# Two of 56 gathered columns per chunk are fetched row by row from SP's and ScalarE's DMA queues

## The chip, the cores and the metric

The kernel runs on one core of one Trainium2 chip. The metric is the device time of that core in microseconds (us); smaller is better. The profiled execution is one run of the same program under the hardware profiler.

## The reference, cut to what matters

A graph of 6250 nodes and 200000 edges, sorted by destination. One small attention layer over the edges (layer 0, with its own scalar weights), then a graph network of three layers of edge attention with 8 heads of 8, all in float32. For the change only the three layers matter:

```
for l in range(3):
    h = layernorm(x)
    q = h[dst] @ Wq;  k = h[src] @ Wkn + edge_attr @ Wke;  v = h[src] @ Wvn + edge_attr @ Wve
    alpha = softmax over the edges of one dst of (q * k).sum per head
    agg   = segment_sum(alpha * v, dst)
    x = x + update(agg, h) @ Wout + MLP(layernorm(x))
```

So each layer needs, for each of the 200000 edges, one row of 128 floats (key and value of the node `src[edge]`), out of a table `tabkv` in DRAM that the layer computes for all nodes.

## The kernel before, in words

The edges are laid out as 128 partitions by 1568 steps (padded): partition p holds 1568 consecutive edges. A layer walks them in 28 chunks (`NCH`) of 56 steps (`C`); a chunk is 128 x 56 edges. Chunks alternate between two buffers, u = 0 and 1. The loop over chunks is written with two chunks in one iteration, on every engine. There are 3 x 28 = 84 such chunks. All orders are written out by hand, engine by engine, with semaphores between them.

For one chunk of a layer:

- **SP (the sync engine)** loads `srcI`, the 128 x 56 source node numbers (L482), once the chunk before in the same buffer has been seen (`seen1`, raised by VectorE as it starts the last slab, L1433); then the spread queries `QQ` (L486, after `q_flat`); then the transposed edge features `EA` (L490, after `done1`).
- **POOL (GpSimd)** issues 56 indirect DMAs, one per step (L546, called from L612 and L614). Each fetches 128 rows of 512 bytes of `tabkv`, one per partition, into column t of `G1[:, u, t, :]`. It may start a buffer when `done1` says that the chunk two before is finished with it.
- **TensorE** computes the edge part of key and value, in 7 slabs (`PT`) of 8 steps (L756).
- **VectorE** first spreads the queries by 8 scans (L1424), then takes the slabs one by one: it waits for the 8 gathers of a slab (L1431), adds the gathered key (L1435) and value (L1436), multiplies with the query (L1438). After the seventh slab come the reduction over heads (L1441), a running maximum, the weights, the weighted value (L1454) and nine scans of running sums (L1461), which end in `done1`.
- **ScalarE** flattens the queries of the next chunk (`query`, L959; it waits until VectorE has finished the seventh slab of this chunk), takes three exponentials (L967 to L969), waits for `done1`, copies the states into `S1` (L973) and issues their store to DRAM (L975). `edges1` is this sequence for one chunk.

Around the 28 chunks stand, in each layer, the computation of the table, a scatter of the queries by 49 indirect DMAs of POOL (L599), and the node update behind them.

Of the kernel before, what the change touches and what calls it, by code (L numbers as in the profile page):

```python
# [5 lines left out]
P = 128  # L6
N = 6250
# [35 lines left out]
B_PE, B_ACT, B_DVE = 11, 8, 5  # L43
HALVES = (range(0, 3), range(3, NB))

PD_RP, PD_END = 6, 7
# [10 lines left out]
def build(nc, A, out):  # L57
# [28 lines left out]
    with ctx:  # L86
# [3 lines left out]
        def sem(name):  # L90
            return ctx.enter_context(nc.semaphore(name))
# [85 lines left out]
        ea_in = [sem(f"ea_in{u}") for u in range(2)]  # L177
        got1 = [[sem(f"got1_{u}_{k}") for k in range(PT)] for u in range(2)]
        seen1 = sem("seen1")
        done1 = sem("done1")  # L180
# [123 lines left out]
        al1 = sb("al1", [P, H, CX])  # L304
        qb = sb("qb", [P, D])

        G1f = G1[:, :, :, :].rearrange("p u c w -> p (u c w)")
# [20 lines left out]
        def hold(eng, passed, s, value):  # L328

            eng.wait_ge(s, value)  # L330
            eng.sem_inc(passed, 1)
# [5 lines left out]
        def _(sp):  # L337
# [118 lines left out]
            with sp.Fori(0, L) as l:  # L456
# [23 lines left out]
                def sources(c, u):  # L480
                    sp.wait_ge(seen1, l * NCH + c + 1)
                    sp.dma_start(srcI[:, u, :], src_pt[:, bass.ds(c * C, C)]).then_inc(idx1[u], 16)  # L482

                def queries(c):
# [11 lines left out]
                for u in range(2):  # L496
                    sources(u, u)
                    features(u, u)
                table_weights(l + 1)
                hold(sp, waits_sp, q_put, (l + 1) * (16 * NT))  # L500
                hold(sp, waits_sp, q_first, (l + 1) * 16)
                sp.dma_start(qexp[0:EP, :].rearrange("(p t) d -> p t d", p=P)[:, 0, :], qb[:, :]).then_inc(q_done, 16)
                hold(sp, waits_sp, q_done, (l + 1) * 16)
                for u in range(2):
                    queries(u)
                with sp.Fori(1, NCH // 2) as i:
                    for u in range(2):
                        sources(2 * i + u, u)
                        queries(2 * i + u)
                        features(2 * i + u, u)  # L510

                store_fixed(st1, R1, l + 1)
# [18 lines left out]
        def _(pool):  # L531
# [62 lines left out]
            with pool.Fori(0, L) as l:  # L594
# [12 lines left out]
                with pool.Fori(0, NCH // 2) as i:  # L607
                    for u in range(2):
                        c = 2 * i + u
                        pool.wait_ge(idx1[u], l * (NCH // 2 * 16) + i * 16 + 16)  # L610
                        hold(pool, waits_pool, done1, l * NCH + c + 1)
                        gathers(u, G1, tabkv, lambda t: got1[u][t // 8], range(C // 2))  # L612
                        hold(pool, waits_pool, kv_ready, (l * NCH + c) * PT + 1)
                        gathers(u, G1, tabkv, lambda t: got1[u][t // 8], range(C // 2, C))  # L614
                fix_and_fetch(st1, R1, l + 1, [(st1_out, (l + 1) * (16 * (NCH + 1)) + 16)], rows1)
# [213 lines left out]
        def _(act):  # L829
# [122 lines left out]
            with act.Fori(0, L) as l:  # L952
# [7 lines left out]

                def edges1(c, u, ahead):

# [5 lines left out]
                    f(score8[:, :, 1:CX], score8[:, :, 1:CX], ACT.Exp, scale=SCALE).then_inc(e1_ready, 1)  # L968
                    f(gate8f, gate8f, ACT.Exp, scale=SCALE).then_inc(e1_ready, 1)  # L969
                    act.wait_ge(done1, n + 3)  # L970
                    act.wait_ge(st1_out, l * (16 * (NCH + 1)) + c * 16 + 16)
                    if ahead:
                        f(S1[:, :, :], SX[:, :, 1:CX].rearrange("p r c -> p c r"), ACT.Copy).then_inc(s_rows, 1)  # L973
                        act.wait_ge(s_rows, n + 2)
                        act.dma_start(chunk_rows(st1, R1, c), S1[:, :, :].rearrange("p c w -> p (c w)")).then_inc(st1_out, 16)  # L975
                    else:
                        f(S1[:, 0:C // 2, :], SX[:, :, 1:1 + C // 2].rearrange("p r c -> p c r"), ACT.Copy).then_inc(s_half, 1)
                        f(S1[:, C // 2:C, :], SX[:, :, 1 + C // 2:CX].rearrange("p r c -> p c r"), ACT.Copy).then_inc(s_rows, 1)
                        act.wait_ge(s_half, l + 2)
                        act.dma_start(chunk_rows(st1, R1, c)[:, 0:C // 2 * R1],  # L980
                                      S1[:, 0:C // 2, :].rearrange("p c w -> p (c w)")).then_inc(st1_out, 16)
                        act.wait_ge(s_rows, n + 2)
                        act.dma_start(chunk_rows(st1, R1, c)[:, C // 2 * R1:C * R1],
                                      S1[:, C // 2:C, :].rearrange("p c w -> p (c w)")).then_inc(st1_out, 16)

                query(l * NCH)
                with act.Fori(0, NCH // 2 - 1) as i:
                    edges1(2 * i, 0, True)
                    edges1(2 * i + 1, 1, True)
                edges1(NCH - 2, 0, True)  # L990
                edges1(NCH - 1, 1, False)
                fix_exp(V1, l + 1, SCALE)
# [21 lines left out]
        def _(dve):  # L1014
# [377 lines left out]
            with dve.Fori(0, L) as l:  # L1392
# [21 lines left out]
                with dve.Fori(0, NCH // 2) as i:  # L1414
                    for u in range(2):
# [12 lines left out]
                        for s in range(PT):  # L1428
                            b = 2 * ((u * PT + s) % 3)
                            steps = slice(8 * s, 8 * s + 8)  # L1430
                            dve.wait_ge(got1[u][s], l * (NCH // 2 * 128) + i * 128 + 128)  # L1431
                            if s == PT - 1:
                                dve.sem_inc(seen1, 1)  # L1433
# [139 lines left out]
```

## Time and profile before

| | us |
|---|---|
| median of 3 runs (9159.09 to 9161.79) | 9159.48 |
| profiled execution, its own time | 9160.98 |
| span of the profiled execution | 9159.2 |
| POOL busy | 6365.8 (70%) |
| VectorE busy | 5799.7 (63%) |
| TensorE busy | 3667.0 (40%) |
| ScalarE busy | 2862.4 (31%) |
| mean busy share of the 16 DMA engines in a stretch of the layers | 0.40 |

Busy time counts the engine's own instructions. Register, branch and semaphore instructions, and the issuing of DMAs on SP's and ScalarE's queues, are not in it; a "q" behind an engine's name (SPq, ACTq) marks its instruction queue, where such issues are listed with a duration.

### The profile page before, as it was taken

The numbers are of one execution on the slowest core, as the hardware profiler recorded it, in microseconds if no ns is written. First come the engines' busy times: TensorE is split into PE (matmuls) and PEld (weight loads), VectorE is DVE, ScalarE is ACT, GpSimd is POOL, SyncE is SP. The second block draws the span as 40 slices with busy tenths as digits, with TensorE's granted clock in tenths as the row PEclk, the third lists the DMA queues.
The fourth block names the chain that finished last, engine by engine and source line by source line (L and its number), as shares of the span: only waits on it lengthen the run. The fifth ranks groups of instructions, "written<-read, shape, count | busy, mean of one in ns | idle before, by whom it ended". The sixth has DMA issues, their size and how long they took to land.

```text
span 9159.2 us, 45368 instructions
## 1 busy us (share of the span) xinstructions
PE 3667.0 (40%) x9857; PEld 2190.5 (24%) x9857; DVE 5799.7 (63%) x6114; ACT 2862.4 (31%) x2181; POOL 6365.8 (70%) x6734
## 2 busy tenths in 40 slices
PE   2677777776323233223342232322242222223325
PEld 1333333333122122212121221222222122212212
DVE  1666666666366776676437667767744776677673
ACT  0566666666122222222222222222221222222223
POOL 6677777774577777777457777777736777777762
PEclk9988888888656566555666665665576656656557
DMA  3455555554433443444234334434314443444331
GB/s 52 161 192 180 186 179 174 175 184 148 132 131 131 139 149 131 139 140 141 64 108 148 132 132 141 147 131 139 125 49 138 139 149 131 137 141 141 131 110 48
DMA packets 405487, 1247.08 MB, mean 136 GB/s; under 512 B 196101, under 2 KB 253910, under 8 KB 360006
## 3 DMA queue, kind: packets, MB, share of 16 engines
q0 software_dynamic: 215104, 429.19, 17.4%
q1 hardware_dynamic: 169606, 468.24, 14.6%
q10 hardware_dynamic: 20736, 349.23, 9.5%
q14 instruction: 31, 0.25, 0.0%
q8 instruction: 10, 0.16, 0.0%
HBM read 808.34 MB, written 437.84 MB: 136 GB/s over the span
## 4 chain that ended last, share of the span: by engine, by line
POOL 52%; issue 20%; PE 17%; ACT 7%; DVE 2%; DMA 1%; DVEq 1%; ACTq 0%; POOLq 0%; SPq 0%
POOL G L546 49%; PE PS L696 7%; PE PS L689 6%; ACT S L910 4%; POOL qexp L599 1%; PE PS L777 1%; POOL QQ L588 1%; PE PS L781 1%; ACT hid L886 1%; PE PS L666 1%; POOL s2exp L565 1%; POOL S L552 1%; POOL G L588 1%; ACT S L851 0%; ACT L855 0%
## 5 line engine op out<-in xcount | busy, mean ns | idle before, releaser
L546 POOL DMA_INDIRECT G<-tabkv,srcI x4704 | 4438.4, 944 | 1433.6 <-issue 1433.6
L756 PE MATMUL PS<-Wkvp,EA 128*128 128x256 f32 x4704 | 1672.9, 531 | 4296.3 <-DVE PX L1438 4217.8
L756 PEld LDWEIGHTS PS<-Wkvp,EA 128*128 128x128 f32 x4704 | 1253.4, 274 | 4716.5 <-DVE PX L1438 4381.7
L546 POOL DMA_INDIRECT G<-tab,srcI x1568 | 1481.4, 945 | 571.9 <-issue 507.2
L959 ACT ACTIVATE QQ<-QQ 128x3584 f32<-128x3584 f32 x84 | 538.4, 6410 | 3313.5 <-DVE PX L1438 3063.1
L1435 DVE TENSOR_TENSOR PS<-PS,G 128x512 f32<-128x512 f32 x588 | 408.4, 695 | 1593.3 <-DMA G<-tabkv,srcI 1575.3
L973 ACT ACTIVATE S<-SX 128x4480 f32<-128x4480 f32 x81 | 663.7, 8194 | 1238.4 <-DVEq L1462 1238.4
L689 PE MATMUL PS<-xT,W1p 128*128 128x512 f32 x1568 | 768.5, 636 | 252.2 <-ACT xT L847 243.1
L1424 DVE TENSOR_TENSOR_SCAN QQ<-PS,QQ 128x456 f32<-128x456 f32 x672 | 679.4, 1082 | 207.9 <-ACT QQ L959 192.3
L1461 DVE TENSOR_TENSOR_SCAN SX<-PS,SX 128x456 f32<-128x456 f32 x756 | 763.2, 1082 | 12.2
L696 PE MATMUL PS<-hid,W2p 128*128 128x512 f32 x1568 | 710.9, 596 | 34.2 <-ACT hid L886 31.5
L1438 DVE TENSOR_TENSOR PX<-PS,QQ 128x512 f32<-128x512 f32 x588 | 624.6, 1062 | 43.8
L886 ACT ACTIVATE hid<-PS,b1c 128x512 f32<-128x512 f32 x784 | 489.1, 684 | 300.6 <-PE PS L689 300.6
L1454 DVE TENSOR_TENSOR SX<-G,PS 128x3584 f32<-128x3584 f32 x84 | 525.7, 6258 | 87.8 <-ACT PS L968 87.8
L689 PEld LDWEIGHTS PS<-xT,W1p 128*128 128x128 f32 x1568 | 318.7, 205 | 660.4 <-issue 396.8
L1436 DVE TENSOR_TENSOR G<-PS,G 128x512 f32<-128x512 f32 x588 | 399.4, 679 | 0.0
L696 PEld LDWEIGHTS PS<-hid,W2p 128*128 128x128 f32 x1568 | 284.4, 190 | 342.0 <-issue 227.7
L910 ACT ACTIVATE S<-S 128x7336 f32<-128x7336 f32 x27 | 360.5, 13352 | 0.0
L599 POOL DMA_INDIRECT qexp<-PX,startI x147 | 140.9, 958 | 312.2 <-DVEq L1412 268.3
L1441 DVE TENSOR_REDUCE al<-PX 128x448 f32<-128x3584 f32 x84 | 326.6, 3888 | 7.7
L666 PE MATMUL PS<-ident,xe 128*128 128x128 f32 x784 | 132.0, 296 | 363.0 <-DVE xe L1188 363.0
L894 ACT ACTIVATE eaC<-PS,b2c 128x512 f32<-128x512 f32 x196 | 134.7, 687 | 418.8 <-PE PS L696 418.8
(311 smaller groups left out, 4090.8 us busy)
## 6 DMA issues: line engine op xcount, KB each, us to landing
st<-S ACTq DMA_DIRECT2D x81, 2240.0 KB, 7.8
EA<-eaT SPq DMA_DIRECT2D x84, 1792.0 KB, 7.8
QQ<-qexp SPq DMA_DIRECT2D x84, 1792.0 KB, 7.3
st<-S ACTq DMA_DIRECT2D x27, 3668.0 KB, 12.0
G<-tabkv,srcI POOLq DMA_INDIRECT x4704, 2.5
xe<-in_edge_attr SPq DMA_DIRECT2D x28, 1792.0 KB, 8.1
qexp<-zeros SPq DMA_DIRECT2D x28, 1792.0 KB, 12.6
eaT<-eaC ACTq DMA_DIRECT2D x28, 1792.0 KB
```

What stands on the lines that cost most here:

```text
L546: nc.gpsimd.indirect_dma_start(out=G[:, u, t, :], out_offset=None, in_=tab[:, :], in_offset=IND(ap=srcI[:, u, t:t + 1], axis=0)).then_inc( ...
L689: last = mm(PS[:, 1 + 2 * r + kh, :], W1p[:, r, kh, :], xT8[:, :], start=True, stop=True)
L696: last = mm(PS[:, 5, :], W2p[:, kh, r, :], hid8[:, r, kh, :], start=(r == 0 and kh == 0), stop=(r == 1 and kh == 1))
L756: last = mm(PS[:, b + j // 2, 2 * P * (j % 2):2 * P * (j % 2) + 2 * P], EA[:, u, 4 * s + j, :], Wkvp[:, :], start=True, stop=True)
L886: f(hid8[:, r, kh, :], PS[:, 1 + 2 * r + kh, :], ACT.Relu, bias=b1c[:, kh:kh + 1]).then_inc(m_act, 1)
L910: f(S0r[:, :, :], SY[:, :, 1:CX].rearrange("p r c -> p c r"), ACT.Copy).then_inc(s0_rows, 1)
L959: f(Qf[:, :, 1:CX], Q1.rearrange("p c d -> p d c"), ACT.Copy).then_inc(q_flat, 1)
L973: f(S1[:, :, :], SX[:, :, 1:CX].rearrange("p r c -> p c r"), ACT.Copy).then_inc(s_rows, 1)
L1424: scan(rows, gate8f, rows, 0.0, ALU.mult, ALU.add)
L1438: tt(PR[:, steps, :], kv_of(b)[:, :, 0:D], Qf[:, :, 1 + 8 * s:9 + 8 * s].rearrange("p d t -> p t d"), ALU.mult).then_inc(kv_used, 1)
L1454: tt(SX[:, 2 * H:R1, 1:CX].rearrange("p (j h) x -> p j h x", h=H), G1[:, u, :, D:2 * D].rearrange("p t (h d) -> p d h t", h=H), score8[:, ...
L1461: scan(rows, gate8f, rows, 0.0, ALU.mult, ALU.add)
```

## The change

POOL gathers columns 0 to 53 of each chunk (`PLAIN = C - 2 = 54`). Column 54 is fetched by SP and column 55 by ScalarE's queue, each with 128 plain DMAs, one per partition, of one row of 512 bytes. The DRAM address of each is computed from a node number that the engine reads into a register: 16 numbers by one call of `values_load_multi_w_load_instructions`, so 8 such calls and 128 DMAs per engine and chunk. To have the numbers in one partition, SP fetches for each chunk two more small arrays `lastI` (128 numbers each). The rows of a chunk are cut into quarters of 32. The quarters 0 to 2 of chunk c + 2 are issued in the iteration of chunk c, by ScalarE behind the store of the states and by SP behind the load of the features; quarter 3 of chunk c + 1 is issued in the iteration of chunk c too, by ScalarE right behind the three exponentials and by SP right behind the load of the queries. Ahead of the loop, both engines issue all four quarters of chunk 0 (SP before it stores `qb` and loads the first queries, ScalarE before its first `query`) and three of chunk 1. VectorE waits, ahead of the seventh slab, for the six gathers left in it and for the eight row semaphores.

```diff
+QUARTER = P // 4
+PLAIN = C - 2
+LAST_GOT = 16 * (PLAIN - 8 * (PT - 1))
...
                 def sources(c, u):
                     sp.wait_ge(seen1, l * NCH + c + 1)
                     sp.dma_start(srcI[:, u, :], src_pt[:, bass.ds(c * C, C)]).then_inc(idx1[u], 16)
+                    for e in range(2):
+                        sp.dma_start(lastI[0:1, u, e, :], src_pt[:, bass.ds(c * C + PLAIN + e, 1)].rearrange("p o -> o p"),
+                                     allow_slow_non_contiguous=True).then_inc(last_in[u], 16)
+
+                def plain_rows(u, i, quarters):
+
+                    hold(sp, waits_sp, last_in[u], l * (NCH // 2 * 32) + i * 32 + 32)
+                    for q in quarters:
+                        for p0 in range(q * QUARTER, (q + 1) * QUARTER, 16):
+                            _, nodes = nc.values_load_multi_w_load_instructions(
+                                lastI[0:1, u, 0, p0:p0 + 16], engines=(mybir.EngineType.SP,), min_val=0, max_val=NP - 1,
+                                skip_runtime_bounds_check_because="src holds node numbers below N")
+                            for p, node in enumerate(nodes, p0):
+                                sp.dma_start(G1[p:p + 1, u, PLAIN, :], tabkv[bass.ds(node, 1), :]).then_inc(plain_got[0][u][q], 16)
...
                 table_weights(l + 1)
+                plain_rows(0, 0, range(4))
                 hold(sp, waits_sp, q_put, (l + 1) * (16 * NT))
...
                 for u in range(2):
                     queries(u)
+                plain_rows(1, 0, range(3))
                 with sp.Fori(1, NCH // 2) as i:
                     for u in range(2):
                         sources(2 * i + u, u)
                         queries(2 * i + u)
+                        plain_rows(1 - u, i - 1 + u, range(3, 4))
                         features(2 * i + u, u)
+                        plain_rows(u, i, range(3))
+                plain_rows(1, NCH // 2 - 1, range(3, 4))
...
-                        gathers(u, G1, tabkv, lambda t: got1[u][t // 8], range(C // 2, C))
+                        gathers(u, G1, tabkv, lambda t: got1[u][t // 8], range(C // 2, PLAIN))
...
     # ScalarE, edges1; its plain_rows is SP's with act, column PLAIN + 1 and plain_got[1]
                     f(gate8f, gate8f, ACT.Exp, scale=SCALE).then_inc(e1_ready, 1)
+                    if ahead:
+                        plain_rows(1 - u, i + u, range(3, 4))
                     act.wait_ge(done1, n + 3)
...
                         act.dma_start(chunk_rows(st1, R1, c), S1[:, :, :].rearrange("p c w -> p (c w)")).then_inc(st1_out, 16)
+                        if two_ahead:
+                            plain_rows(u, i + 1, range(3))
...
+                for k in range(2):
+                    hold(act, waits_act, a_out[k], (l + 1) * (16 * ((NB + 1 - k) // 2)))
+                hold(act, waits_act, h_out, (l + 1) * 32)
+                plain_rows(0, 0, range(4))
                 query(l * NCH)
+                plain_rows(1, 0, range(3))
...
-                            dve.wait_ge(got1[u][s], l * (NCH // 2 * 128) + i * 128 + 128)
-                            if s == PT - 1:
+                            if s < PT - 1:
+                                dve.wait_ge(got1[u][s], l * (NCH // 2 * 128) + i * 128 + 128)
+                            else:
+                                dve.wait_ge(got1[u][s], l * (NCH // 2 * LAST_GOT) + i * LAST_GOT + LAST_GOT)
+                                for q in range(4):
+                                    for e in range(2):
+                                        dve.wait_ge(plain_got[e][u][q], l * ROW_SEM + i * (16 * QUARTER) + 16 * QUARTER)
                                 dve.sem_inc(seen1, 1)
```

## Rows read from the trace of the kernel before

**Rows 1.** The page's costliest groups: busy, mean ns | idle before, releaser.
```profile
L546 POOL DMA_INDIRECT G<-tabkv,srcI x4704 | 4438.4, 944 | 1433.6 <-issue 1433.6
L1435 DVE TENSOR_TENSOR PS<-PS,G 128x512 f32<-128x512 f32 x588 | 408.4, 695 | 1593.3 <-DMA G<-tabkv,srcI 1575.3
```

**Rows 2.** Timeline of SP's queue, four periods of a layer: start us, us, queue.
```profile
3038.53 0.34 SPq L482 DMA_DIRECT2D srcI<-in_src  x1
...
3318.17 0.34 SPq L482 DMA_DIRECT2D srcI<-in_src  x1
```

**Rows 3.** Timeline of ScalarE over one chunk.
```profile
3740.16 6.45 ACT L959 ACTIVATE QQ<-QQ 128x3584 f32<-128x3584 f32 x1 [37.17 <-DVE PX L1438]
...
3748.10 0.54 ACT L967 ACTIVATE SX<-PS 128x448 f32<-128x448 f32 x1 [1.49 <-DVE PS L1452]
...
3749.00 0.52 ACT L969 ACTIVATE PS<-PS 128x456 f32<-128x456 f32 x1
...
3764.79 8.19 ACT L973 ACTIVATE S<-SX 128x4480 f32<-128x4480 f32 x1 [15.28 <-DVEq L1462]
...
3773.14 0.34 ACTq L975 DMA_DIRECT2D st<-S  x1
```

**Rows 4.** Timeline of VectorE behind the seventh slab and into the next chunk.
```profile
3739.07 1.06 DVE L1438 TENSOR_TENSOR PX<-PS,QQ 128x512 f32<-128x512 f32 x1
...
3755.51 9.08 DVE L1461 TENSOR_TENSOR_SCAN SX<-PS,SX 128x456 f32<-128x456 f32 x9
...
3774.98 0.68 DVE L1435 TENSOR_TENSOR PS<-PS,G 128x512 f32<-128x512 f32 x1
...
3777.30 0.69 DVE L1435 TENSOR_TENSOR PS<-PS,G 128x512 f32<-128x512 f32 x1
...
3779.64 0.69 DVE L1435 TENSOR_TENSOR PS<-PS,G 128x512 f32<-128x512 f32 x1
```

**Rows 5.** Timeline of SP's queue at the program's start (L392: one row, 320 bytes).
```profile
12.94 0.52 SPq L389 DMA_DIRECT2D st<-zeros  x1
...
13.94 1.12 SPq L391 DMA_DIRECT2D st<-zeros  x1
15.10 0.26 SPq L392 DMA_DIRECT2D st<-zeros  x1
15.40 0.25 SPq L393 DMA_DIRECT2D st<-zeros  x1
```

**Rows 6.** Timeline of SP's queue, DMAs back to back, address from a register.
```profile
6922.73 0.55 SPq L365 DMA_DIRECT2D Wqkv<-in_Wvn  x1
6923.38 0.54 SPq L383 DMA_DIRECT2D bqkv<-in_bq  x1
...
6925.23 0.38 SPq L383 DMA_DIRECT2D bqkv<-in_bke  x1
6925.71 0.38 SPq L383 DMA_DIRECT2D bqkv<-in_bve  x1
```

**Rows 7.** All instructions of L482: durations min/median/max in ns.
```profile
L482 SPq FUSED_REGOPS  x78: 37/37/42, 2549.1 to 8768.7; - x78
L482 SPq MOVE srcI<-in_src x78: 29/29/29, 2549.2 to 8768.7; - x78
```

**Rows 8.** All DMAs of L486 and L502, and for L502 the time to landing.
```profile
L486 SPq DMA_DIRECT2D QQ<-qexp x84: 332/333/343, 2480.7 to 8777.8; - x84
...
L502 SPq DMA_DIRECT2D qexp<-qb x3: 343/344/354, 2479.1 to 6951.0; - x3
...
DMA to landing us min/median/max: 1.5/1.5/1.6
```

**Rows 9.** Timeline of all engines at the start of the third layer's chunks.
```profile
6914.39 1.19 SPq L490 DMA_DIRECT2D EA<-eaT  x1
...
6949.81 0.97 POOL L546 DMA_INDIRECT G<-tabkv,srcI  x1 [0.30 <-issue]
...
6952.64 14.11 SPq L486 DMA_DIRECT2D QQ<-qexp  x2
...
6960.14 6.25 ACT L959 ACTIVATE QQ<-QQ 128x3584 f32<-128x3584 f32 x1 [83.56 <-DMA QQ<-qexp]
...
7023.63 6.39 ACT L959 ACTIVATE QQ<-QQ 128x3584 f32<-128x3584 f32 x1 [57.24 <-DVE PX L1438]
```

More of the change, by code:

```diff
@@ L44 @@
 HALVES = (range(0, 3), range(3, NB))
+QUARTER = P // 4
+ROW_SEM = 16 * QUARTER * (NCH // 2)
+PLAIN = C - 2
+LAST_GOT = 16 * (PLAIN - 8 * (PT - 1))
 PD_RP, PD_END = 6, 7
@@ L178, in build @@
         got1 = [[sem(f"got1_{u}_{k}") for k in range(PT)] for u in range(2)]
+        last_in = [sem(f"last_in{u}") for u in range(2)]
+        plain_got = [[[sem(f"plain_got{u}_{q}_{e}") for q in range(4)] for u in range(2)] for e in ("sp", "act")]
+        waits_act = sem("waits_act")
         seen1 = sem("seen1")
@@ L305, in build @@
         qb = sb("qb", [P, D])
+        lastI = sb("lastI", [1, 2, 2, P], i32)
         G1f = G1[:, :, :, :].rearrange("p u c w -> p (u c w)")
@@ L959, in query, with plain_rows, edges1 @@
                     f(Qf[:, :, 1:CX], Q1.rearrange("p c d -> p d c"), ACT.Copy).then_inc(q_flat, 1)
-                def edges1(c, u, ahead):
+                def plain_rows(u, i, quarters):
+                    hold(act, waits_act, last_in[u], l * (NCH // 2 * 32) + i * 32 + 32)
+                    for q in quarters:
+                        for p0 in range(q * QUARTER, (q + 1) * QUARTER, 16):
+                            _, nodes = nc.values_load_multi_w_load_instructions(
+                                lastI[0:1, u, 1, p0:p0 + 16], engines=(mybir.EngineType.Activation,), min_val=0, max_val=NP - 1,
+                                skip_runtime_bounds_check_because="src holds node numbers below N")
+                            for p, node in enumerate(nodes, p0):
+                                act.dma_start(G1[p:p + 1, u, PLAIN + 1, :], tabkv[bass.ds(node, 1), :]).then_inc(plain_got[1][u][q], 16)
+                def edges1(c, u, ahead, i, two_ahead):
                     n = l * NCH + c
@@ L984, in edges1 @@
                                       S1[:, C // 2:C, :].rearrange("p c w -> p (c w)")).then_inc(st1_out, 16)
+                for k in range(2):
+                    hold(act, waits_act, a_out[k], (l + 1) * (16 * ((NB + 1 - k) // 2)))
+                hold(act, waits_act, h_out, (l + 1) * 32)
+                plain_rows(0, 0, range(4))
                 query(l * NCH)
+                plain_rows(1, 0, range(3))
                 with act.Fori(0, NCH // 2 - 1) as i:
[L988 to L991, printed above, removed]
+                    edges1(2 * i, 0, True, i, True)
+                    edges1(2 * i + 1, 1, True, i, True)
+                edges1(NCH - 2, 0, True, NCH // 2 - 1, False)
+                edges1(NCH - 1, 1, False, NCH // 2 - 1, False)
                 fix_exp(V1, l + 1, SCALE)
```

## The prediction

> **What bounds the kernel now.** I read the page's groups first. POOL's gathers of the layers are the largest: 4704 of them, 944 ns busy each, and 1433.6 us of idle time before them, all put down to issue, so POOL waits for nobody [rows 1]. That is (4438.4 + 1433.6) / 4704 = 1.248 us per gather. Then I took the period of a chunk from SP's queue: four periods are 3318.17 - 3038.53 = 279.64 us, so 69.9 us each [rows 2], and 56 x 1.248 = 69.9. POOL's issue is the whole period; VectorE waits for gathers, 1575.3 us in all [rows 1].
>
> Next, how much room the other engines have. VectorE ends the seventh slab at 3740.13 (call it T), its nine scans at 3764.6, begins the next slabs at 3774.98 and takes one per 2.33 us when nothing is missing [rows 4], so it could have the next T at 3774.98 + 7 x 2.33 = 3791.3, 51 us after this one. ScalarE [rows 3] works 6.45 (queries), three exponentials ending at 3749.52, 8.19 (states) and 0.34 (store), and sits idle 37.17 us before the queries and 15.28 us before the states. SP's queue does three DMAs per chunk. So without two gathers POOL's period would be 67.4 us, and VectorE allows it.
>
> **The change, part by part.**
>
> *POOL.* Two gathers fewer: 2 x 1.248 = 2.5 us per chunk, 84 chunks: -210 us, if nothing else becomes longer than 67.4 us.
>
> *ScalarE's queue.* It gains 128 DMAs and 8 register loads per chunk, issued in order between its activations; a DMA issue holds the queue. Call x the all-in time per row. When ScalarE is the one that is late, its loop over one chunk is: queries 6.45, exponentials 1.42, 32 rows beside the 15.27 us that VectorE needs up to `done1` (hidden while 32x stays under 15.27), states and store 8.19 + 0.15 + 0.34, small gaps 0.1 [rows 3], then 96 rows with nothing of its own chain beside them. A = 31.9 + 96x. Behind the waiting rows stand the next chunk's queries and exponentials, on which VectorE waits. The question is whether A stays below 67.4 (x below 0.370) or at least below 69.9 (x below 0.396).
>
> *The price x.* The trace has no row DMA into SBUF from a register address, and no register load at all. Issue: a single-row DMA took 0.26 us, next one 0.30 us after it (L392), two earlier single-row ones 0.52 and 1.12 [rows 5]. A 128-row DMA takes 0.333 alone [rows 8]. With a register address, DMAs back to back follow with a gap of 0.10 (6925.23 + 0.38 to 6925.71) [rows 6], in which 37 + 29 ns of register operations lie [rows 7]. So one row costs 0.26 + 0.10 = 0.36 from the nearest kind, 0.43 if it costs what 128 rows do, and 0.64 by L365's rows (0.55 and the gap). I take 0.36: L392 is the same shape, and L389 and L391 stand behind a large store. Register load of 16: below, one register operation, 0.03 us (x = 0.36), or 16 of them, 0.46 us (x = 0.385); above, a round trip of a small DMA, 1.5 us [rows 8] (x = 0.45). A load must bring its values back before the next instruction, so it is nearer to a round trip; I take 1.25 us, 0.08 per row: x = 0.435.
>
> Two of the pages bear on that load. The Trainium skill says in "Runtime: NRT & Kernel Launch" (Instruction fetch mechanics) that loading sequencer registers from HBM costs about 200 ns per register even in bulk; taken for these loads from SBUF as an estimate that is 3.2 us per 16, x = 0.56 and, by the sum below, about 10560 us. In "DMA: Bandwidth & Descriptors" (Latency and other measured facts) it gives a floor of about 600 ns for such a load, which would make x = 0.395 and leave the time where it was. No row of this trace shows either.
>
> *The sum.* A = 31.9 + 96 x 0.435 = 73.7 us, 3.8 longer than now. 32x = 13.9 is hidden.
>
> *SP.* 128x = 55.7 plus five DMAs (three as now, two of `lastI` like L365's at 0.6) is about 58 us, under 73.7: not a bound. Its order: the rows stand before the feature load and the next sources; features are needed a chunk later, sources 67 us later, and queries are asked for at T + 6.4. Cost nothing; that cover would be gone at x above 0.5, when ScalarE is worse anyway.
>
> *The start of a layer* [rows 9]. SP is done with its loads at 6926.1; with four more small loads at 6928.6; 128 rows bring it to 6984.3; `qb` goes out and lands 1.5 us later, so the first queries are asked for at 6986 instead of 6952.6 and land 7.5 us later. ScalarE's flatten ends at 6999.8, VectorE's scans and seven slabs put the first T at 7026 instead of 7023.6. ScalarE then issues 96 rows and is free at 7041.6. From the start of its loop to the next T there are 7.9 + 15.3 + 10.2 + 16.4 = 49.8 us [rows 3, 4]. So the last T of the layer is at 7041.6 + 26A + 49.8; now it is 7023.6 + 27 x 69.9. The difference is 26 (A - 69.9) - 2.1: with A = 73.7, +96.7 us per layer, three layers +290. That is against the profiled execution, 9161.0: 9451 us. It stands 1.5 us above the median of the runs, so nothing to correct.
>
> *VectorE* gets eight more waits per chunk. They are passed long before where ScalarE is early; their handling lies in VectorE's free 16 us (67.4 - 51). Nothing. The DMA engines carry 256 packets of 512 bytes in place of two gathers' worth of the same bytes; nothing at this share (0.40 busy).
>
> **The rivals.**
>
> *Cheap rows (the other side): faster.* The place is the same 96 rows of ScalarE, behind the states' store. If x is below 0.370 (row 0.36, load under 0.2 us, or a row cheaper than L392's), A stays below 67.4 and POOL remains the bound: -210 us and a few us of start, 8955 us. Between 0.370 and 0.396 a part is left: x = 0.385 gives A = 68.9, -28 per layer, 9077 us. For it: one register address costs 66 ns only, and 0.26 is the duration of L392 and of L393 [rows 5, 7]. Against it: every register load must cost nearly nothing. It decides at x = 0.396.
>
> *Dear rows.* The issue costs what a 128-row DMA does, 0.43 + 0.08 = 0.51. Then 32 rows no longer hide: A = 16.6 + 128 x 0.51 = 81.9, +310 per layer, 10090 us. The same follows from a row at 0.36 and a load of 2.4 us, that is if each of the 16 values makes a trip of its own. For it: all isolated DMAs with registers are 0.333 or more [rows 8], and values may be read one by one. The page's 200 ns per register belongs here too.
>
> *Very dear rows.* L365's pace, 0.64 + 0.08 = 0.72 [rows 6]: A = 108.8, +1009 per layer, 12190 us. For it: DMAs in bursts there cost 0.55 where isolated ones cost 0.33, and the change is one long burst from two queues at once. Against it: L392 and L393 stand back to back at 0.30 [rows 5].
>
> *It does not do what it says*: POOL's gathers become slower by contention with the row DMAs, so that 54 take 69.9 us. 1.248 is steady under all present traffic [rows 1]; I give it no chance of its own.
>
> **How the numbers follow.** Forecast (A from 70.4 to 79, +40 to +650 us): 0.36. Cheap rows, whole or partly: 0.31. Dear rows, up to +1500: 0.19. Very dear: 0.10. In between, within 0.2% of before (about what a measurement of this kernel can tell from no change): 0.04. Faster 0.31, same 0.04, slower 0.65. The range runs from the full gain, 8950, to 10500: it leaves out the very dear rows and some of the dear ones. The forecast's own range is 9200 to 9810.
>
> **What would show it.** ScalarE's queue with 128 DMAs per chunk at 0.36 us spacing within a 16 and a pause of 1.25 us between them; the period of L973 at 73.7 us against POOL's 67.4 of issue and 6 us of waiting for `done1`; ScalarE's idle time before L959 gone. The forecast is wrong if the period is 67.4 and POOL still has no wait but issue, or if rows come at 0.5 us or more.

## The result: 12% slower, and the profile after

| | us |
|---|---|
| before, median of 4 runs (9158.25 to 9161.79) | 9159.28 |
| after, median of 4 runs (10278.35 to 10286.43) | 10283.02 |
| after over before, 95% interval | 1.1226 (1.1207 to 1.1246) |
| profiled execution of after, its own time | 10286.43 |

The change costs 1124 us where 290 were forecast. These are lines of the page of the changed kernel: the chain by engine and line, then costliest groups (busy, mean ns | idle before, releaser).

```profile
span 10284.6 us, 112432 instructions
...
ACTq 37%; PE 15%; issue 13%; ACT 13%; DVE 8%; DVEq 7%; POOL 3%; SPq 2%; DMA 1%; POOLq 0%
ACTq L997 28%; ACTq L993 9%; PE PS L723 7%; DVEq L1514 6%; ACT S L1013 6%; PE PS L716 5%; DVE SX L1506 5%; ACT S L937 3%; DVE SX L1513 1%; SPq L504 1%; PE PS L804 1%; POOL QQ L615 1%; PE PS L808 1%; ACT hid L913 1%; POOL G L573 1%
...
L573 POOL DMA_INDIRECT G<-tabkv,srcI x4536 | 4279.6, 943 | 2612.5 <-issue 1351.9
...
L1506 DVE TENSOR_TENSOR SX<-G,PS 128x3584 f32<-128x3584 f32 x84 | 525.8, 6259 | 2701.4 <-ACT PS L1006 2701.4
L986 ACT ACTIVATE QQ<-QQ 128x3584 f32<-128x3584 f32 x84 | 524.4, 6243 | 4648.3 <-issue 4267.0
```

The gathers (L573) take 943 ns each, as before, and are the 168 fewer that the change asks for, but of POOL's 2612.5 us of idle time before them only 1351.9 are still issue [rows 1]: POOL waits now. VectorE waits 2701.4 us for ScalarE's exponential (L1006) ahead of the weighted value (L1506), where the kernel before has 87.8 us (L1454 there):

```profile
L1454 DVE TENSOR_TENSOR SX<-G,PS 128x3584 f32<-128x3584 f32 x84 | 525.7, 6258 | 87.8 <-ACT PS L968 87.8
```

ScalarE sits idle 4267.0 us before the queries (L986) and no engine releases it there: its own queue is busy, with the rows (L997, 28% of the chain) and the register loads (L993, 9%). This is ScalarE's timeline over one chunk, which answers to [rows 3]:

```profile
4007.46 6.26 ACT L986 ACTIVATE QQ<-QQ 128x3584 f32<-128x3584 f32 x1 [52.01 <-issue]
4009.01 4.76 ACTq L997 DMA_DIRECT2D G<-tabkv  x12
4013.63 0.52 ACT L1005 ACTIVATE SX<-PS 128x448 f32<-128x448 f32 x1
...
4014.51 0.49 ACT L1007 ACTIVATE PS<-PS 128x456 f32<-128x456 f32 x1
4014.70 8.46 ACTq L997 DMA_DIRECT2D G<-tabkv  x18
4030.29 8.19 ACT L1013 ACTIVATE S<-SX 128x4480 f32<-128x4480 f32 x1 [15.29 <-DVEq L1514]
4038.64 0.39 ACTq L1015 DMA_DIRECT2D st<-S  x1
4042.86 47.16 ACTq L997 DMA_DIRECT2D G<-tabkv  x96
4092.82 6.24 ACT L986 ACTIVATE QQ<-QQ 128x3584 f32<-128x3584 f32 x1 [54.33 <-issue]
```

From the store at 4038.64 to the next queries at 4092.82 there are 54.2 us, in which 96 rows with their six loads are issued and nothing else. The part from the queries to the store takes 31.2 us, as the prediction had it. The loop is then 85.4 us here and 83.0 us in the next chunk. This loop, from one copy of the states (L1013, before: L973) to the next, is the period of a chunk. Over the 78 periods inside the layers it is 84.14 us on the mean (69.90 before, worked out from all executions of the copy). The whole difference can be laid out from these: 6563.3 - 5452.2 = 1111.1 us in the periods, +23.7 up to the first of them, +8.8 between the layers, -18.1 behind the last; together 1125.5, which is the difference of the two spans (10284.63 and 9159.15).

What the rows and loads cost, by their lines in the trace (durations min/median/max in ns; L997 and L993 on ScalarE's queue, L504 and L500 on SP's):

```profile
L997 ACTq FUSED_REGOPS  x10752: 37/37/37, 2445.8 to 10002.2; - x200
L997 ACTq MOVE G<-tabkv x10752: 29/29/29, 2445.8 to 10002.2; - x200
L997 ACTq DMA_DIRECT2D G<-tabkv x10752: 228/235/1085, 2445.9 to 10002.3; - x200
...
L993 ACTq TENSOR_LOAD <-lastI x672: 1191/1304/3646, 2444.5 to 9994.4; - x168
```
```profile
L504 SPq DMA_DIRECT2D G<-tabkv x10752: 224/225/1167, 2456.9 to 9994.2; - x200
...
L500 SPq TENSOR_LOAD <-lastI x672: 1133/1232/3922, 2455.4 to 9986.3; - x168
```

A row is 0.037 + 0.029 for its address and 0.235 for the DMA, and with the three gaps between these instructions the next row starts 0.391 us later (median). The load of 16 takes 1.304 us; the forecast had 1.25.

### The profile page after: what moved, and what is told of

Its sections match the earlier page's. It is cut to its first block, busy times and chain, and to the rows that moved or that the text cites. A ratio compares the mean times of both kernels' runs of the same rounds, so it can differ in the third digit from the quotient of the medians.

```text
span 10284.6 us, 112432 instructions
## 1 busy us (share of the span) xinstructions
PE 3287.2 (32%) x9857; PEld 1953.7 (19%) x9857; DVE 5779.7 (56%) x6114; ACT 2839.8 (28%) x2181; POOL 6208.8 (60%) x6566
## 4 chain that ended last, share of the span: by engine, by line
ACTq 37%; PE 15%; issue 13%; ACT 13%; DVE 8%; DVEq 7%; POOL 3%; SPq 2%; DMA 1%; POOLq 0%
ACTq L997 28%; ACTq L993 9%; PE PS L723 7%; DVEq L1514 6%; ACT S L1013 6%; PE PS L716 5%; DVE SX L1506 5%; ACT S L937 3%; DVE SX L1513 1%; SPq L504 1%; PE PS L804 1%; POOL QQ L615 1%; PE PS L808 1%; ACT hid L913 1%; POOL G L573 1%
## 5 line engine op out<-in xcount | busy, mean ns | idle before, releaser
L573 POOL DMA_INDIRECT G<-tabkv,srcI x4536 | 4279.6, 943 | 2612.5 <-issue 1351.9
L783 PE MATMUL PS<-Wkvp,EA 128*128 128x256 f32 x4704 | 1299.9, 439 | 5856.5 <-DVE PX L1490 5771.7
L783 PEld LDWEIGHTS PS<-Wkvp,EA 128*128 128x128 f32 x4704 | 1019.1, 222 | 6138.0 <-DVE PX L1490 5884.9
L1506 DVE TENSOR_TENSOR SX<-G,PS 128x3584 f32<-128x3584 f32 x84 | 525.8, 6259 | 2701.4 <-ACT PS L1006 2701.4
L573 POOL DMA_INDIRECT G<-tab,srcI x1568 | 1481.7, 945 | 567.2 <-issue 510.7
L986 ACT ACTIVATE QQ<-QQ 128x3584 f32<-128x3584 f32 x84 | 524.4, 6243 | 4648.3 <-issue 4267.0
L1013 ACT ACTIVATE S<-SX 128x4480 f32<-128x4480 f32 x81 | 663.7, 8193 | 1239.2 <-DVEq L1514 1239.2
```

Of the source, the lines that this page charges most:

```text
L573: nc.gpsimd.indirect_dma_start(out=G[:, u, t, :], out_offset=None, in_=tab[:, :], in_offset=IND(ap=srcI[:, u, t:t + 1], axis=0)).then_inc( ...
L783: last = mm(PS[:, b + j // 2, 2 * P * (j % 2):2 * P * (j % 2) + 2 * P], EA[:, u, 4 * s + j, :], Wkvp[:, :], start=True, stop=True)
L1506: tt(SX[:, 2 * H:R1, 1:CX].rearrange("p (j h) x -> p j h x", h=H), G1[:, u, :, D:2 * D].rearrange("p t (h d) -> p d h t", h=H), score8[:, ...
```

## The experiments

The later runs were made on seven chips. On five of them the kernel before itself took 10846 to 10868 us, on the two others 9158 to 9160 us; no chip showed both, and what differs between them is not known. Each comparison is with the kernel before on the same chip, and only those beside 9159 us are used for sizes.

**POOL's part by itself.** The kernel before with the last two gathers of each chunk left out, and with `G1` cleared once ahead of the layers, which is not in the diff shown.

```diff
-                        gathers(u, G1, tabkv, lambda t: got1[u][t // 8], range(C // 2, C))
+                        gathers(u, G1, tabkv, lambda t: got1[u][t // 8], range(C // 2, C - 2))
```

> The kernel before with 54 gathers per chunk and nothing in place of the last two (their columns hold stale rows; G1 is cleared once, some 8 us). Theory: what the change could win at most is 2 x 1.248 us per chunk, 84 chunks, 210 us: 10650 where the kernel before takes 10855. Rival (something else paces the chunks on this chip, so that fewer gathers win nothing): 10850 or more.

Measured: 8954.21 us, 0.9775 (0.9759 to 0.9792). The page's group and two executions of the states' copy in ScalarE's timeline:

```profile
L546 POOL DMA_INDIRECT G<-tabkv,srcI x4536 | 4280.3, 944 | 1382.2 <-issue 1382.2
...
3993.55 8.19 ACT L973 ACTIVATE S<-SX 128x4480 f32<-128x4480 f32 x1 [15.29 <-DVEq L1467]
...
4060.93 8.19 ACT L973 ACTIVATE S<-SX 128x4480 f32<-128x4480 f32 x1 [15.30 <-DVEq L1467]
```

The period is 4060.93 - 3993.55 = 67.4 us and POOL waits for nothing but issue. So the removed gathers bring 204 us (9158.37 - 8954.21) where the forecast had 210, in a kernel that also clears `G1` once (6.7 us of VectorE), and what the fetching adds is about 1124 + 204 = 1328 us.

**POOL out of the way.** The changed kernel with only 7 of the 54 gathers of a chunk, one per slab. VectorE's waits are set to match, which the diff leaves out.

```diff
-                        gathers(u, G1, tabkv, lambda t: got1[u][t // 8], range(C // 2))
+                        gathers(u, G1, tabkv, lambda t: got1[u][t // 8], range(0, C // 2, 8))
...
-                        gathers(u, G1, tabkv, lambda t: got1[u][t // 8], range(C // 2, PLAIN))
+                        gathers(u, G1, tabkv, lambda t: got1[u][t // 8], range(C // 2 + 4, PLAIN, 8))
```

> The changed kernel, but POOL issues only 7 of its 54 gathers per chunk, one per slab, so that its gathers are out of the way (most edges get a stale row; G1 is cleared once, some 8 us). Theory (ScalarE's queue is the bound by its own instructions; what lengthens it further on this chip is POOL's gathers in flight): the period falls from 134.2 us in the changed kernel on this chip to 82 to 85 us, the 84.1 us of the first measurement, and the time from 15580 to about 11300. Rival (the rows themselves are slow on this chip): period stays over 120 us. Rival (POOL's gathers were part of the bound of 84.1 us too): period under 78 us.

Measured: 10232.16 us, 1.117 (1.1152 to 1.1189). Its gathers, POOL's busy tenths, and ScalarE's 96 rows:

```profile
POOL 7677777753000000001300000000040000000001
...
L573 POOL DMA_INDIRECT G<-tabkv,srcI x588 | 554.5, 943 | 6163.3 <-DVEq L1516 4165.8
...
4033.24 46.58 ACTq L997 DMA_DIRECT2D G<-tabkv  x96
```

POOL is nearly silent in the layers and the 96 rows still take 46.6 us; the period is 83.51. The period of 82 to 85 us held; the total in the expectation was that for the chips on which the kernel before takes 10850 us. Neither POOL's gathers nor contention of their transfers with the rows makes the loop: ScalarE's own stream of instructions does, but for 0.6 us of 84.1.

**Which rows count.** 32 rows more beside the stretch in which ScalarE waits for VectorE, 32 fewer behind the store: 64 and 64.

```diff
-                        plain_rows(1 - u, i + u, range(3, 4))
+                        plain_rows(1 - u, i + u, range(2, 4))
...
-                            plain_rows(u, i + 1, range(3))
+                            plain_rows(u, i + 1, range(2))
```

> 64 of ScalarE's rows ahead of its wait for done1, 64 behind the store; base 10283 us. Theory (its own order is the bound): 10.4 us more than is free there, 16.8 saved behind the store, period 78 us, 9800 us. Rival (only the sum of the rows counts): 10283.

Measured: 9719.76 us, 1.0611 (1.0593 to 1.0629), period 77.26. ScalarE's timeline:

```profile
4033.30 6.24 ACT L986 ACTIVATE QQ<-QQ 128x3584 f32<-128x3584 f32 x1 [36.00 <-issue]
...
4040.54 24.41 ACTq L997 DMA_DIRECT2D G<-tabkv  x50
4065.20 8.24 ACT L1013 ACTIVATE S<-SX 128x4480 f32<-128x4480 f32 x1 [24.36 <-issue]
...
4077.51 31.46 ACTq L997 DMA_DIRECT2D G<-tabkv  x64
```

The 64 rows beside VectorE now end at 4064.95, so that the copy of the states (L1013) waits 24.36 us and for issue, no longer for VectorE; about 9 us of them lie on the path (the part from the queries to the store is 40.3 us for 31.2) and the rest, some 23, stays hidden. Behind the store 32 rows fewer save 16 us (36.95 for 52.96); the sum is the 7 us by which the period is shorter. The rival, that only the number of rows counts, fell. In the changed kernel the rows beside VectorE are free, as forecast, because VectorE needs its 15.3 us and the rows begin already while the queries are being flattened.

**Half as many rows.** One column of 128 rows, of which SP's queue fetches 64 and ScalarE's 64 (32 behind the store, 32 beside VectorE); POOL gathers 55. The diff shows SP's start and ScalarE's rows behind the store.

```diff
-PLAIN = C - 2
+PLAIN = C - 1
...
-                plain_rows(0, 0, range(4))
+                plain_rows(0, 0, range(2))
...
-                            plain_rows(u, i + 1, range(3))
+                            plain_rows(u, i + 1, range(2, 3))
```

> One column, 64 rows by SP and 64 by ScalarE, POOL gathers 55; for a chip on which the kernel before takes 9158 us. Theory: ScalarE's loop is 84.1 - 64 x 0.52 = 51 us, SP's under 40, POOL's 68.7 holds: 9158 - 105 = 9053 us. Rival (rows cost something by being there): 9158 or more.

Measured: 9050.62 us, 0.9879 (0.9863 to 0.9896). It is 1.2% faster than the kernel before. The group of the gathers, the chain by engine, and ScalarE's timeline:

```profile
POOL 52%; issue 20%; PE 17%; ACT 7%; DVE 2%; DMA 1%; DVEq 1%; ACTq 0%; POOLq 0%; SPq 0%
...
L571 POOL DMA_INDIRECT G<-tabkv,srcI x4620 | 4359.3, 944 | 1408.8 <-issue 1408.8
...
4023.09 15.70 ACTq L995 DMA_DIRECT2D G<-tabkv  x32
4055.01 6.37 ACT L984 ACTIVATE QQ<-QQ 128x3584 f32<-128x3584 f32 x1 [35.88 <-DVE PX L1488]
```

POOL is the bound again, at 55 x 1.248 = 68.6 us (measured 68.66), and ScalarE, done with its 32 rows at 4038.8, waits again for VectorE until 4055.01. One gather per chunk is worth 109 us when the rows are hidden.

**The parts of the price.** Two kernels take parts of a row's cost away. In the first the rows come from addresses known at compile time: no load, no address operations. The diff is ScalarE's; SP's is the same with its own addresses.

```diff
-                            _, nodes = nc.values_load_multi_w_load_instructions(
-                                lastI[0:1, u, 1, p0:p0 + 16], engines=(mybir.EngineType.Activation,), min_val=0, max_val=NP - 1,
-                                skip_runtime_bounds_check_because="src holds node numbers below N")
-                            for p, node in enumerate(nodes, p0):
-                                act.dma_start(G1[p:p + 1, u, PLAIN + 1, :], tabkv[bass.ds(node, 1), :]).then_inc(plain_got[1][u][q], 16)
+                            for p in range(p0, p0 + 16):
+                                act.dma_start(G1[p:p + 1, u, PLAIN + 1, :], tabkv[41 * p:41 * p + 1, :]).then_inc(plain_got[1][u][q], 16)
```

> 256 row DMAs per chunk at constant addresses, no loads, no arithmetic (the two columns hold wrong rows). Theory: 0.30 us per row (as e4's trace shows between POOL's bursts), 96 of them 29 us, ScalarE's loop 31.9 + 29 + some 3 for store and loop end = 64 us, POOL's 67.4 us bound: 8955 us. Rival (row DMAs as such are the bound): near 10280.

Measured: 9176.46 us, 1.0016 (1.0006 to 1.0026), where the theory said 8955. In the second only the first load of each call is kept, and its 16 numbers serve for all rows of the call.

```diff
-                            _, nodes = nc.values_load_multi_w_load_instructions(
...
+                            if p0 == quarters[0] * QUARTER:
+                                _, nodes = nc.values_load_multi_w_load_instructions(
...
```

> One load of 16 numbers per call of plain_rows, reused (wrong rows for most edges); base 10283 us. Theory: 5 loads fewer behind the store, 5 x 1.53 = 7.7 us, period 76.5, 9680 us. Rival (the loads are not on the path): 10283.

Measured: 9238.12 us, 1.0079 (1.0062 to 1.0095), where the theory said 9680. Both miss, and in opposite directions. All the DMAs of the rows, and two runs of 96 rows behind the store, first of the kernel with constant addresses:

```profile
L991 ACTq DMA_DIRECT2D G<-tabkv x10752: 215/283/4347, 2448.5 to 8891.0; - x200
...
4004.99 36.04 ACTq L991 DMA_DIRECT2D G<-tabkv  x96
...
4072.97 40.51 ACTq L991 DMA_DIRECT2D G<-tabkv  x96
```

and then of the kernel with one load per call:

```profile
L999 ACTq DMA_DIRECT2D G<-tabkv x10752: 222/228/1092, 2444.4 to 8971.2; - x200
L999 ACTq FUSED_REGOPS  x2640: 37/37/37, 2444.2 to 8964.9; - x189
...
4025.73 36.51 ACTq L999 DMA_DIRECT2D G<-tabkv  x96
...
4062.53 6.24 ACT L987 ACTIVATE QQ<-QQ 128x3584 f32<-128x3584 f32 x1 [39.98 <-issue]
```

What each interval between starts on ScalarE's queue came to, from the store to the next queries, mean over the chunks inside the layers (worked out from the starts of the instructions; the row interval behind a load holds the load):

```
                         after          one load per call    constant addresses
row to row           90 x 0.426 = 38.3   95 x 0.373 = 35.4    95 x 0.393 = 37.3
over a load           6 x 1.837 = 11.0    1 x 2.503 =  2.5    none
row to load           5 x 0.264 =  1.3    none                none
store to first; last row to queries  2.3  2.5                 1.8
all                              53.0    40.4                39.1
```

With one load per call the 16 registers recur, and the program computes the address of a repeated one only once: its FUSED_REGOPS are 2640 in place of 10752. The stretch is 12.5 us shorter. The theory had 7.7 of these: five loads and the slower row behind each. It had not that the load behind the store would be shorter too, 2.35 us on the mean in place of 3.33 (1.0), nor the two rows behind that load (1.0), and nothing for the missing address operations, which the remaining 2.8 or so are put down to.

With constant addresses half of ScalarE's rows come 0.314 us or less after the one before, and yet the mean behind the store is 0.393: the DMA instructions themselves grow, to a median of 283 ns and up to 4347, where with address operations between them the median was 235. They don't grow evenly. From 4 to 8 us after the start of the states' store ScalarE's rows are 0.305 us apart on the mean, from 12 to 16 us 0.763, and from 20 us on 0.37 to 0.45; SP's rows slow down in the same microseconds (0.77 to 1.05 from 4 to 16 us). So 0.393 is the mean of this kernel and not a floor that one queue has by itself. The other queue's rows are not needed for it either: with none of SP's issued within 1.5 us, ScalarE's still come 0.374 us apart. The same kernel on the other chips shows SP's rows 0.30 us apart where neither a row of ScalarE's nor a gather is issued within 1.5 us, 0.35 with ScalarE's rows near, and 0.43 with both (all worked out from the starts of the instructions). What holds the issue back was not separated further; a kernel with one queue at constant addresses was not run. At its mean ScalarE's loop is 31.2 + 39.1 = 70.3 us (the period is 70.53), above POOL's 67.4: even rows without any load or address did not make this split faster than before.

**On the chips where the kernel before takes 10850 us.** The same kernels there, and one queue at a time: ScalarE alone with one column, and SP alone with one column (POOL gathers 55). The diff is the first one's, which takes SP's calls away; the other takes ScalarE's.

```diff
-                        plain_rows(1 - u, i - 1 + u, range(3, 4))
...
-                        plain_rows(u, i, range(3))
...
-                                    for e in range(2):
+                                    for e in (1,):
```

> SP's column goes back to POOL (55 gathers, 68.7 us per chunk); ScalarE keeps its 128 rows. Theory (ScalarE's own queue is the bound, 84.2 us per chunk in the changed kernel): same period, 10280 us. Rival (the two queues slow each other, or all rows crowd on shared DMA hardware): rows get cheaper with one queue alone, period under 80 us, under 9950 us.

> ScalarE's column goes back to POOL (55 gathers, 68.7 us); SP keeps 128 rows. Theory: SP's queue needs 8 loads and 128 rows, 67.0 us at the changed kernel's means (0.433 us per row, 1.45 per load), and some 3.7 us of other DMAs, waits and loop end: 70.7 us per chunk, about 9225 us (9160 to 9300). Rival (SP has room, as the prediction had it): POOL's 68.7 us hold, 9055 us. Rival (SP is a second bound near 84 us): over 10000 us.

The split column and the constant addresses, whose diffs stand above, were run with these two for the first time:

> One column only, 64 of its rows by SP and 64 by ScalarE (32 beside VectorE's chain, 32 behind the store of the states); POOL gathers 55. Theory: ScalarE's loop is about 84.2 - 64 rows x 0.52 = 51 us plus waits, SP's under 40, both under POOL's 68.7: 1.25 us per chunk are won, 9160 - 105 = 9055 us. Rival (plain rows cost something by merely being there, contention or waits of VectorE): no gain, 9160 or more.

> All 256 row DMAs stay, but at constant addresses of the table: no register loads, no address arithmetic (the two columns hold wrong rows). Theory (the price is load plus arithmetic plus issue, 0.52 us per row, of which the DMA itself is 0.235 and a gap): ScalarE's loop falls to about 60 us, POOL's 67.4 us bound again, 8955 us. Rival (the row DMAs themselves, their descriptors or landing, are the bound): stays near 10280 us.

The next runs were to tell whether the chip or the kernels made these times: the two kernels of the case again, and the experiments again.

> The kernel before, unchanged, with its trace, beside which all experiments are now read: it took 10846 us in two sets of experiments and 9159 us in the first measurement. If the sequencers' records there come 0.70 us apart in long stretches, as in e1's trace, the difference of 1690 us is in those stretches; if not, the DMAs or the clock are slower. If the time is 9159 us again, the set is comparable with the first measurement.

> The changed kernel, unchanged, as the base for the experiments on this chip. If it is near 10283 us, the set compares directly. If it is far above (e1 with half of its row DMAs took 15000 us), the same cause that lengthens the kernel before by 1690 us lengthens long runs of sequencer instructions, and the experiments must be read against this run.

> The kernel of e1 again, for the same reason. Theory (ScalarE's queue alone is the bound): 10280 us, 84 us per chunk. Rival (the two queues slow each other): under 9950 us.

> The kernel of e3 again, since in its first run the kernel before took 10846 us beside it and not 9159, so that neither theory could be read. Theory: both queues are under POOL's 68.7 us per chunk, 9055 us. Rival (plain rows cost something by being there): 9160 or more.

> The kernel of e4 again (256 row DMAs per chunk at constant addresses, so the two columns hold wrong rows), for the same reason. Theory (load and arithmetic are half of the price): about 60 us on ScalarE, POOL's 67.4 us bound, 8955 us. Rival (the row DMAs themselves are the bound): near 10280 us.

And the first runs of one load per call, and of 64 rows behind the store and 64 beside VectorE:

> Row DMAs with register addresses as in the change, but only one load of 16 numbers per call of plain_rows, reused for all its rows (wrong rows for most edges): 4 loads per chunk and engine fewer on the average, of 1.30 us and 0.23 us on the first row behind each. Theory (loads are part of ScalarE's 84.2 us): behind the store 5 loads fewer, 7.7 us, period 76.5 us, 10283 - 78 x 7.7 = 9680 us where the kernel before takes 9159; where it takes 10850, at least 600 us under the changed kernel's 15580. Rival (rows' issue waits for the DMA hardware, not for the loads): less than 200 us.

> ScalarE issues 64 rows (not 32) before it waits for done1, and 64 (not 96) behind the store. Theory (ScalarE's own order is the bound; 23 us lie free there from the start of the queries to done1): 64 rows take 33.4 us, 10.4 more than is free, but 16.8 are saved behind the store: period 84.2 - 6.3 = 78, about 9800 us where the kernel before takes 9159. Rival (only the sum of the rows counts): no change, 10283.

Measured:

```
                              us        over before (95% interval)
before again               10868.15    1.00 (10856 beside it)
after again                15582.34    1.4352 (1.4311 to 1.4394)
ScalarE's column alone     14993.57    1.3832 (1.3808 to 1.3855); again 1.3838 (1.3815 to 1.3862)
SP's column alone          15002.15    1.3828 (1.3805 to 1.3851); again 1.3909 (1.3886 to 1.3932)
64 and 64 behind/beside    14783.34    1.3630 (1.3607 to 1.3653)
one load per call          14318.86    1.3198 (1.3176 to 1.3220)
one column split           12968.17    1.1962 (1.1943 to 1.1982); again 1.1964 (1.1943 to 1.1984)
constant addresses         12911.15    1.1911 (1.1891 to 1.1931); again 1.1922 (1.1902 to 1.1942)
```

A run of the changed kernel there, ScalarE's queue:

```profile
L997 ACTq DMA_DIRECT2D G<-tabkv x10752: 2/235/1509, 3304.7 to 15285.0; - x200
...
6006.24 6.24 ACT L986 ACTIVATE QQ<-QQ 128x3584 f32<-128x3584 f32 x1 [104.55 <-issue]
6007.91 4.62 ACTq L997 DMA_DIRECT2D G<-tabkv  x11
...
6041.59 97.64 ACTq L997 DMA_DIRECT2D G<-tabkv  x96
6139.50 6.24 ACT L986 ACTIVATE QQ<-QQ 128x3584 f32<-128x3584 f32 x1 [102.23 <-issue]
```

The rows beside the queries come 11 in 4.62 us, as fast as elsewhere (12 in 4.76), the 96 behind the store in 97.6 us in place of 47. In the first stretch POOL is waiting, in the second it gathers. In all runs of this kind that fetch rows there are stretches in which the instructions of the two queues come 0.7 or 1.4 us apart, and they lie beside POOL's gathers. An interval between two of ScalarE's rows with no gather starting within 1.5 us of it had a median of 0.390 us in that run, one with a gather 2.1 us. That the gathers cause it is not shown: no kernel without them was run on such a chip.

ScalarE's column alone answers to the rival that the two queues slow each other. Where no gather was near, its rows came 0.535 us apart on the mean with SP silent and with SP issuing alike, so the rival finds nothing there; over the whole chunk the period fell from 134.2 to 127.0 us. The totals can't tell for the chips beside 9159 us.

The split column, 1.2% faster beside 9159, is 20% slower here, and constant addresses, no change there, are 19% slower. Among the kernels that fetch rows these two change places in the order, and the kernel before is ahead of both.

A last run of SP's column alone, meant for a chip where the kernel before takes 9159 us, met the other kind:

> SP fetches one column (128 rows and 8 loads per chunk), ScalarE's queue fetches nothing, POOL gathers 55 columns. Theory (the price of a row is the same on SP's queue, and SP's 128 rows are its own loop): in the changed kernel SP issued its rows in stretches of 14.4 and 50.1 us per chunk, and its other work and waits for itself came to about 7 us, so one turn of SP takes 70 to 72 us, against POOL's 55 x 1.248 = 68.6. The period is then 70.0 to 72.0 and the time 9170 to 9330, ScalarE's queue having none of it. Rival 1 (the prediction's figure, SP takes about 58 us): POOL stays the bound, period 68.7, time 9055, as with the column split between the queues. Rival 2 (two queues slow each other, so one alone is quick): rows at 0.36 or less, period 68.7 as well, but the spacing of rows would show it.

15115.19 us; so whether SP alone would be a bound there stays open as a total.

## Why the prediction was wrong

**POOL's gain: right.** 210 forecast, 204 measured with the two gathers left out.

**The mechanism: right.** ScalarE's loop of 31.9 + 96x was forecast; 31.2 + 53.0 was measured, with nothing in the second term but the stretch from the store to the queries; the 96 rows are on the path and the 32 are not, shown by moving 32 of them; a chunk's period sets 1111 of the 1125 us. Put into the prediction's own sum, the measured A of 84.14 gives 26 x 14.24 - 2.1 = 368 us per layer and 10265 us in all, beside 10286 of the profiled execution. The side on which it would fall was the likelier of the two given (0.65).

**The price x: wrong, and this is the step that failed.** It was 0.435, of which 0.36 for a row and 0.08 for its share of a load. By the table above, 16 rows with their load take 15 x 0.426 + 1.837 + 0.264 = 8.49 us, 0.530 each; with what stands at the end of the stretch, (84.1 - 31.9) / 96 = 0.544. A was 10.4 us short by it, 811 us over 78 periods, of the 834 us by which the change cost more than the 290 forecast. The forecast's own range, 9200 to 9810, ended below the measured time. This is the term of the rival "dear rows" (0.51 and more, chance 0.19), whose price came true though not its form: it had the 32 rows on the path too. The 10.4 us of A that were missing (84.1 less 73.7):

- The row. Its DMA cost 0.235, even less than the 0.26 of [rows 5]. But the gap of 0.10 from [rows 6] was misread: the prediction put both register operations of [rows 7] into it, 37 + 29 ns, and the trace of the kernel before has only the one of 29 ns there. These DMAs have no address to compute:

```profile
L383 SPq DMA_DIRECT2D bqkv<-in_bve x4: 381/382/432, 28.0 to 6925.7; - x4
...
L383 SPq MOVE bqkv<-in_bve x3: 29/29/29, 2456.2 to 6925.6; - x3
```

  A row of the change has both, so that 0.156 lies between the end of one DMA and the start of the next, two operations of 66 ns and three gaps of 30. Median 0.391 where 0.36 was forecast: 3.0 us per chunk.
- The load, 1.304 for 1.25: 0.3 us. The estimate between a register operation and a round trip was good. The Trainium skill's 200 ns per register ("Runtime: NRT & Kernel Launch", Instruction fetch mechanics) would be 3.2 us; this load is from SBUF and took 0.08 per register. The Trainium skill's floor of about 600 ns ("DMA: Bandwidth & Descriptors", Latency and other measured facts) is passed by a factor of two.
- The row behind a load costs 0.23 more than another (0.624 us to the next, 0.391 otherwise, medians): six times 0.23, 1.4 us. Not in the forecast.
- The load behind the states' store takes 3.33 us on the mean of 78 in place of 1.30, and the two intervals from the second and the third row behind it 0.91 and 0.87 in place of 0.39: 3.0 us. The forecast priced each instruction as if it stood alone. The place in the queue is not what makes this load slow, for SP's queue shows the same in the same microsecond. These are ScalarE's load behind the store of 4038.64, SP's load of that moment, and SP's load right behind its own DMA of 128 rows, the features:

```profile
L993 ACTq TENSOR_LOAD <-lastI x1: 3252/3252/3252, 4039.2 to 4039.2; - x1
...
L500 SPq TENSOR_LOAD <-lastI x1: 2692/2692/2692, 4038.9 to 4038.9; - x1
...
L500 SPq TENSOR_LOAD <-lastI x1: 1134/1134/1134, 4030.8 to 4030.8; - x1
```

  Of SP's 672 loads 75 begin 0.2 to 0.9 us after ScalarE's store, and they take 3.26 us on the mean; none of the other 597 takes more than 1.8. What a load meets there stays open.
- Pauses of about 0.3 us, three in each burst: 0.8 us. And 2.4 us at the end of the loop's body in every second chunk (2.8 us from the last row to the queries at 4092.82, where 0.58 is usual): 1.1 us per chunk. This one explains why the periods alternate, 85.4 and 83.0. Neither was in the sum.

Together these are 9.6 of the 10.4 us; the rest is not placed.

**SP: a size off.** It was put at 58 us per chunk. This is the timeline of its queue:

```profile
4015.70 14.36 SPq L504 DMA_DIRECT2D G<-tabkv  x32
4030.28 0.36 SPq L512 DMA_DIRECT2D EA<-eaT  x1
4032.08 50.09 SPq L504 DMA_DIRECT2D G<-tabkv  x96
4085.09 0.37 SPq L490 DMA_DIRECT2D srcI<-in_src  x1
4085.65 1.31 SPq L492 DMA_DIRECT2D lastI<-in_src  x2
4099.22 0.36 SPq L508 DMA_DIRECT2D QQ<-qexp  x1
```

The rows alone are 14.36 + 50.09 us. From the queries' load at 4013.88 to the end of the small loads at 4086.96 SP issues for 73.1 us, of which 2.9 are the pause at the loop's end; only then, until 4099.22, does it wait for ScalarE. SP is hidden behind ScalarE's 84 us, but had ScalarE's rows been cheap, SP's 71 to 73 would have stood above POOL's 67.4. The rival "cheap rows" needed both queues below that, and in it the prediction weighed ScalarE's alone. That SP would then be the bound is worked out, not shown.

**VectorE's waits and the transfers: right**, at nothing: without POOL's gathers 0.6 us of the period went. **The layers' starts and ends** came to 14.4 us together (23.7 up to the first period, 8.8 over the two changes of layer, 18.1 given back behind the last), 4.8 per layer where the forecast had -2.1.

**Three small sums** of the prediction are off, and none of them moves a side: sixteen register operations (0.46 us) make x 0.389 and not 0.385; A = 79 gives +700 us and not +650; x = 0.56 gives 10590 us and not 10560, since the 32 rows no longer hide there.

**The range** held the time (8950 to 10500). It held only because it reached up into the dear rows, and not by the term that was forecast.

## What to carry to other kernels

Before a burst of small instructions is put on a queue, write down the whole row of instructions that one element needs, with the gap between each two of them (here 30 ns, three times), read from a DMA that has the same ones ahead of it (here the gap of a DMA with one register operation was taken for one with two). Look also at what another DMA does to the first of them: here the load was 2.0 us dearer beside the start of a store, on either queue. A price from the nearest DMA in the trace is only one of the terms. Then give the burst only the time in which that engine waits anyway: here 64 rows per chunk and queue were hidden and one gather was gained, 128 were not and 12% were lost. Where the margin between gain and loss is 0.03 us per element, as here (0.370 and 0.396), the forecast has to cover the same sum on every engine that takes a share.

## What was not expected of the hardware

- Rows of 512 bytes at constant addresses came 0.314 us or less apart in half of the cases, but 0.393 on average behind the store, with slow stretches on both queues at once (0.763 on ScalarE's from 12 to 16 us after the store).
- A register load of 16 numbers took 1.30 us (1.23 on SP), and 3.3 us where it began in the first microsecond after the start of ScalarE's store of the states, on the queue that issued the store and on the other alike.
- Rows on one queue were as dear with the other queue silent: ScalarE's column alone, on a chip of the slower kind, had a median spacing of 0.391 and loads of 1.30 us, as in the changed kernel there.
- On five of the seven chips of the later runs the instructions of SP's and ScalarE's queues came in stretches 0.7 or 1.4 us apart beside POOL's gathers, so that the same change costs 12% on one chip and 44% on another. The kernel before is slower there in other ways: its DMA of `srcI` was issued in 0.337 us as elsewhere but landed after 9.7 us where it was 1.8, its period is 79.09 us for 69.90, and 899 us are lost ahead of the first period.
